# Filler matmuls in the waits of TensorE, and the output bias as a 128-row product, in a fused state-space, attention and feed-forward layer

## The reference

```python
x = x + ssm(_layernorm(x), W_in, conv_w, ..., W_out)      # 512 inner channels, 16 states each
x = x + ffn(_layernorm(x), w_gate, w_up, w_down)          # silu(gate) * up, 768 wide
x = x + wkv(_layernorm(x), Wr, br, Wk, ..., Wo, bo, ...)  # 1024 wide
x = x + ffn(_layernorm(x), w_gate, w_up, w_down)
...
h = scan(exp(dt * A), dt * B * xc)                        # along the 512 tokens, per channel and state
y = (einsum('bldn,bln->bld', h, C) + D * xc) * silu(z)    # the sum over the 16 states
...
out = (sigmoid(R) * WKV).reshape(n, t, -1) @ Wo.T + bo
```

## Time and profile before

| | |
|---|---|
| runs | 1724.32 us median (1724.05, 1724.32, 1731.85) |
| the profiled execution | 1725.72 us, span 1723.9 us |
| mean granted clock of PE | 0.933 |
| busy: PE, DVE, POOL, ACT | 85%, 88%, 73%, 70% of the span |
| memory traffic | 225.20 MB, mean 131 GB/s |

### The profile page before, as it was taken

The page is one execution under the profiler, slowest core; times in us unless marked ns, Lnnn a source line. Parts: engine busy times, 40 slices in busy tenths (PEclk is TensorE's granted clock), DMA queues, the critical chain, the costliest instruction groups (busy, mean ns, idle before and its releaser), DMA issues.

```text
span 1723.9 us, 18980 instructions
## 1 busy us (share of the span) xinstructions
PE 1461.0 (85%) x4800; PEld 713.7 (41%) x4800; DVE 1521.4 (88%) x2045; ACT 1211.0 (70%) x1993; POOL 1265.8 (73%) x970
## 2 busy tenths in 40 slices
PE   5245589779999998899799998899989988999987
PEld 2011234234534552354434453354534553546464
DVE  3399989889999999999999999999999999976561
ACT  3647688856698778968598767889688677664621
POOL 0788987987598877988688867998588978742340
PEclk9567689879999999999899999999999998999999
DMA  8535344324345324453345414553435433321211
GB/s 245 200 110 172 134 141 164 127 92 163 97 145 190 115 100 161 157 175 101 104 139 189 138 56 153 197 193 105 134 121 164 132 119 113 102 63 52 83 49 31
DMA packets 163518, 225.20 MB, mean 131 GB/s; under 512 B 13457, under 2 KB 104082, under 8 KB 163410
## 3 DMA queue, kind: packets, MB, share of 16 engines
q1 hardware_dynamic: 163410, 223.99, 40.0%
HBM read 179.90 MB, written 39.85 MB: 127 GB/s over the span
## 4 chain that ended last, share of the span: by engine, by line
PE 39%; DVE 9%; ACT 6%; issue 5%; POOL 5%; DMA 2%; SPq 1%; DVEq 0%; POOLq 0%; ACTq 0%
PE ps_r L1347 24%; PE ps_r L1356 11%; POOL bu L905 3%; PE ps_y L1398 3%; DVE ps_d L1220 2%; ACT ps_d L1064 1%; DVE bu L1227 1%; ACT L947 1%; DVE sums L1314 1%; PE ps_r L1354 1%; DMA win<-w_in_dram 1%; DVE sums L1308 1%; POOL bu L910 1%; DVE bu L1220 1%; DVE ps_r L1299 1%
## 5 line engine op out<-in xcount | busy, mean ns | idle before, releaser
L905 POOL TENSOR_TENSOR bu<-rep,bc 128x512 f32<-128x512 f32 x512 | 651.2, 1297 | 133.0 <-PE ps_y L1398 114.5
L1064 ACT ACTIVATE ps_d<-rep,scale_a 128x512 f32<-128x512 f32 x512 | 338.1, 684 | 178.5 <-DVE bu L1227 163.4
L1220 DVE TENSOR_TENSOR_SCAN ps_d<-ps_d,bu 128x512 f32<-128x512 f32 x384 | 457.8, 1215 | 6.1 <-ACT ps_d L1064 4.5
L1347 PE MATMUL ps_r<-xT,wgu 128*128 128x512 f32 x768 | 353.5, 606 | 19.4 <-ACT hf L1086 4.5
L1347 PE MATMUL ps_r<-mix,wkv 128*128 128x512 f32 x512 | 250.7, 625 | 32.4 <-DVE yr L1329 8.0
L1227 DVE TENSOR_TENSOR bu<-ps_d,bc 128x512 f32<-128x512 f32 x384 | 251.1, 677 | 0.5
L947 ACT ACT_TABLE_LOAD x191 | 245.1, 1283 | 3.4
L1347 PEld LDWEIGHTS ps_r<-xT,wgu 128*128 128x128 f32 x768 | 142.4, 192 | 225.2 <-issue 215.3
L1398 PE MATMUL ps_y<-bu,sel 128*32 128x512 f32 x1024 | 151.5, 666 | 96.2 <-POOL bu L910 52.9
L922 POOL TENSOR_TENSOR kv<-sums,kv 128x1024 f32<-128x1024 f32 x64 | 150.7, 2355 | 83.7 <-DVE sums L1314 83.3
L910 POOL TENSOR_TENSOR bu<-bu,bc 128x512 f32<-128x512 f32 x128 | 162.7, 1273 | 31.5 <-DVE bu L1220 30.8
(11 more groups left out here) (100 smaller groups left out, 2047.7 us busy)
## 6 DMA issues: line engine op xcount, KB each, us to landing
rep<-dd_scratch SPq DMA_DIRECT2D x128, 512.0 KB, 4.9
wgu<-gu_scratch SPq DMA_DIRECT2D x96, 256.0 KB, 3.3
bc<-bc_scratch SPq DMA_DIRECT2D x64, 256.0 KB, 3.9
dd_scratch<-dd SPq DMA_DIRECT2D x32, 512.0 KB, 3.7
win<-w_in_dram SPq DMA_DIRECT2D x64, 128.0 KB, 2.4
wkv<-w_k_dram SPq DMA_DIRECT2D x64, 128.0 KB, 2.8
wkv<-w_v_dram SPq DMA_DIRECT2D x64, 128.0 KB, 3.2
wr<-w_r_dram SPq DMA_DIRECT2D x64, 128.0 KB, 3.2
```

Source lines behind the costliest of these rows:

```text
L905: pool.tensor_tensor(bu[:, i % BU, :], rep[:, g % REP, 1, :], bc[:, 0, q, :], ALU.mult)\
L1064: act.activation(ps_d[D_BANK[i]][:, :], rep[:, g % REP, 0, :], ACT.Exp, scale=scale_a[:, a, NQ * j + q:NQ * j + q + 1]).then_inc(decay_rea ...
L1220: dve.tensor_tensor_scan(states, d[:, :], bu[:, i % BU, :], 0.0, ALU.mult, ALU.add)\
L1347: last = pe.matmul(dst, lhs, rhs, start=n == 0, stop=n == len(pairs) - 1)
```

## The change

A new unit `p_warm` is put into PE's list, 134 times at 49 places, singly or up to 27 in a row. It multiplies `bo_rows` (128x128, zero but for row 64, which is one) with the first 64 columns of the identity, repeated eight times to 512 columns. Row 64 of those columns is zero, so the product is zero. It is added to `ps_y`, in the middle of an accumulation; ahead of the very first group it opens and closes a sum of its own. The bias becomes the product of `bo_rows` with all 128 rows of `wdt_bo`, whose rows from 64 on are cleared first. The tile `ones` is replaced by a column `one`. The other units, on all engines, keep their order.

```diff
-        wdt_bo = sb("wdt_bo", [RANK + 1, DIN])
+        wdt_bo = sb("wdt_bo", [P, DIN])
...
-        ones = sb("ones", [P, P])
+        one = sb("one", [P, 1])
+        bo_rows = sb("bo_rows", [P, P])
...
+                sp.wait_ge(pool_const.sem, 1)
                 sp.dma_start(bo, b_o).then_inc(r_weights_in.sem, 16)
...
+            pool.memset(wdt_bo[RANK:, :], 0.0).then_inc(pool_const.sem, 1)
+            pool.wait_ge(pool_const.sem, 1)
...
-            pool.memset(ones[:, :], 1.0).then_inc(pool_const.sem, 1)
+            pool.memset(one[:, :], 1.0).then_inc(pool_const.sem, 1)
+            pool.memset(bo_rows[:, :], 0.0).then_inc(pool_const.sem, 1)
...
-            pool.wait_ge(pool_const.sem, 6)
+            pool.wait_ge(pool_const.sem, 8)
+            pool.memset(bo_rows[RANK:RANK + 1, :], 1.0).then_inc(pool_const.sem, 1)
+            pool.wait_ge(pool_const.sem, 9)
...
-                    pe.matmul(d, ones[RANK:RANK + 1, 0:P], bo, start=True, stop=False)
+                    pe.matmul(d, bo_rows[:, :], wdt_bo[:, 0:C], start=True, stop=False)
...
+                    elif unit == "p_warm":
+
+                        if groups and groups % NQ == 0:
+                            pe.wait_ge(gated.sem, at(gated, 0, groups // NQ))
+                        pe.matmul(ps_y[:, :].rearrange("p (a b) -> p a b", b=RANK), bo_rows[:, :],
+                                  ident[:, 0:RANK].unsqueeze(1).to_broadcast([P, T // RANK, RANK]),
+                                  start=groups % NQ == 0, stop=groups % NQ == 0)
                     elif unit == "p_y":
 
+                        groups += 1
```

The list of PE changes only by the inserted words; its first line reads after the change:

```diff
-        "hp_turn*2 p_in*5 p_xproj p_in p_dt p_in*2 p_dt*3 p_y hp_turn*2 p_y p_in*4 p_y*5 p_in*2 p_y p_in*2 p_y "
+        "hp_turn*2 p_in*3 p_warm p_in*2 p_warm*2 p_xproj p_in p_dt p_in*2 p_dt*2 p_warm p_dt p_warm*27 p_y p_warm "
```

More of the change, by code:

```diff
@@ L77 @@
     "rp_turn": KC, "rp_turn2": KC, "rp_up": FM, "rs_ffn": FM, "rv_down": 2, "rv_stats": 2, "rv_aggr": 2, "rv_up": FM,
-    "s_out": 1,
+    "s_out": 1, "p_warm": 1000,
 }
@@ L107 @@
[L107 to L116, removed]
@@ new lines @@
+        "hp_turn*2 p_warm*2 p_y p_warm*2 p_in*4 p_y p_warm*5 p_y*2 p_warm*4 p_y p_warm*8 p_y p_in*2 p_warm*2 p_y "
+        "p_in*2 p_y p_warm*3 p_xproj p_y p_warm p_dt*2 p_y p_warm*7 p_y p_dt*2 p_y p_warm*3 hp_turn p_warm*2 "
+        "hp_turn p_y p_warm*4 p_y p_warm*4 p_y p_post p_y p_post p_warm fp_turn p_warm p_y p_warm*3 fp_turn2 "
+        "p_warm fp_turn fp_turn2 p_y fp_gate fp_up fp_gate p_y fp_up fp_gate fp_up fp_gate p_y fp_up fp_gate "
+        "fp_up p_warm p_y p_warm*2 fp_gate fp_up p_y fp_down fp_down2 p_y fp_down fp_down2 p_in*5 p_y p_in "
@@ new lines @@
+        "fp_turn2 p_in p_y p_in*2 p_wo p_wo2 p_in*3 p_y p_xproj p_k p_v p_dt rp_turn rp_turn2 rp_turn rp_turn2 "
+        "p_y p_recept rp_gate rp_up rp_gate rp_up rp_gate rp_up rp_gate p_y p_warm rp_up p_dt p_y rp_gate*2 "
+        "rp_up*2 p_y p_k rp_down rp_down2 rp_down p_y rp_down2 p_v p_y p_recept*2 p_k*2 p_v*2 p_recept p_y "
+        "p_recept*3 p_k p_warm p_v p_k p_recept p_y p_dt p_k p_v p_post*2 p_v p_wo p_wo2 fp_turn fp_turn2 p_y "
+        "fp_turn fp_turn2 p_wo p_wo2 fp_gate fp_up fp_gate p_y fp_up fp_gate fp_up fp_gate fp_up fp_gate fp_up "
@@ new lines @@
+        "p_y fp_gate fp_up p_k p_dt p_y p_v fp_down fp_down2 fp_down fp_down2 hp_turn*2 p_y p_warm p_wo p_wo2 "
+        "p_wo fp_turn fp_turn2 fp_turn fp_turn2 p_wo2 p_in*2 p_k p_y p_warm p_y p_warm p_in rp_turn rp_turn2 "
+        "rp_turn rp_turn2 p_in*2 p_v p_in*3 p_y p_xproj p_dt p_k p_y p_recept*3 p_v p_k p_v p_dt p_y rp_gate "
+        "p_warm rp_up p_warm p_recept p_y rp_gate rp_up p_k p_v p_recept rp_gate rp_up p_y p_recept rp_gate rp_up "
+        "rp_gate rp_up p_y rp_gate p_recept rp_up p_k p_y rp_down p_v p_recept rp_down2 rp_down p_y rp_down2 p_k "
@@ new lines @@
+        "p_v p_y p_wo p_k p_wo2 p_post*2 p_y p_v p_wo p_wo2 p_dt fp_turn fp_turn2 fp_turn fp_turn2 p_k fp_gate*2 "
+        "fp_up*2 p_y fp_gate fp_up fp_gate fp_up p_y fp_gate fp_up p_dt p_y p_v fp_gate fp_up p_y fp_down "
+        "fp_down2 fp_down hp_turn*2 fp_down2 p_warm p_y p_in p_wo p_wo2 p_y p_wo p_in p_wo2 fp_turn fp_turn2 "
+        "fp_turn fp_turn2 p_in*2 p_warm*2 p_in p_y rp_turn rp_turn2 rp_turn rp_turn2 p_in*2 p_y p_k p_xproj p_v "
+        "p_y p_dt p_in p_recept p_y p_k p_v p_recept*2 rp_gate p_k rp_up p_y rp_gate rp_up p_v p_recept rp_gate "
@@ L443, in full_counts @@
     for seq, unit, i in order("p"):
-        if unit == "p_y" or unit in SECOND.values():
+        if unit in ("p_y", "p_warm") or unit in SECOND.values():
             continue
@@ L1044, in run @@
                             act.wait_ge(m_full.sem, FULL[m, "p_in", 2 * JD - 1])
-                        act.activation(rest_u, dd_slot(i)[:, 1, :], ACT.Identity, bias=ones[:, 0:1]).then_inc(sp_u.sem, 1)
+                        act.activation(rest_u, dd_slot(i)[:, 1, :], ACT.Identity, bias=one[:, 0:1]).then_inc(sp_u.sem, 1)
                         act.wait_ge(sp_u.sem, at(sp_u, m, i + 1))
@@ L1048, in run @@
                         act.wait_ge(sp_ln.sem, at(sp_ln, m, i + 1))
-                        act.activation(rest_u, rest_u, ACT.Identity, bias=ones[:, 0:1], scale=-1.0).then_inc(sp_neg.sem, 1)
+                        act.activation(rest_u, rest_u, ACT.Identity, bias=one[:, 0:1], scale=-1.0).then_inc(sp_neg.sem, 1)
                     elif unit == "a_decay":
@@ L1361, in run @@
             def run(units):
-                dst = {}
+                dst, groups = {}, 0
                 for t, unit, i in units:
```

78 lines of the change are left out of this document (36 added, 42 removed).

## The result

| | before | after |
|---|---|---|
| median of four executions each, taken together | 1727.13 us (1724.05 to 1731.85) | 1701.14 us (1700.30 to 1701.96) |
| ratio | | 0.9847, 95% interval 0.9819 to 0.9875 |
| the profiled execution | 1725.72 us, span 1723.9 | 1701.39 us, span 1699.6 |
| mean granted clock | 0.933 | 0.982 |
| time at the half level, from the clock records | 231.5 us | 62.6 us |

The kernel is 26 us shorter than before by the medians, and 24.3 us between the two profiled executions.

The account below looks back on a forecast made before the run. DVE was taken to bound the long stretch to 1520 us, PE the last. From the profiled 1725.7 us, 1.0 overrun was added, 11.5 clock and 4.1 bias taken off: 1711 us, range 1698 to 1721.

Parts of the forecast that it names:

- The overrun term: Places where a filler ends after the work it stands before is ready: 1 us in all, bounds 0 and 10.
- The clock term: DVE's waits for PE behind half-clock stretches, 80 to 1520 us: full clock wins 11.5 us, ends 0 and 19.4.
- two in or just behind a dip that gets a filler: From 460 to 1520 us, two DVE waits for PE of 1.5 and 2.6 us, 4.1 together, counted as removable.
- six tenths: Share of the 19.4 us of removable waits taken as won, 11.5 us; part would return as waits for POOL or ACT.
- The bias term: 32 biased output tiles, each 0.39 us shorter with the full product: 4.1 us won, ends 0 and 7.2.
- I take 2.5 us: DVE's 11 waits for xk at biased tiles, 5.6 us from 460 to 1520 us: 2.5 us of them won.
- save nothing: In the last stretch, the last four biased tiles, followed by a 4.06 us wait for DVE, win no time.
- The first, off the path: In the long DVE stretch, removed waits for PE become waits for POOL or ACT: 1720 us, chance 0.19.
- The second: Zeros or 32-column groups fail to hold the clock; the first p_y starts 25 us later: 1751 us, chance 0.05.
- The third: Clock held in large gaps only, dips left from 100 to 200 us; half of 11.5 us comes: 1717 us, chance 0.08.
- The fourth: Fillers anywhere delay real work by more than they win, the exposed end of the bounds: 1734 us, chance 0.02.
- What would show it: Signs to check in the new profile: clock, PE busy time, first p_y, biased tile, DVE's waits, last stretch.

Follow-up runs that it names:

- The run with 54 fillers: The changed kernel with 54 instead of 27 fillers ahead of the first p_y: 1719.93 us, ratio 0.9967.
- early and bias: The changed kernel with the 128-row bias and only the 88 fillers up to the 22nd p_y group: 1706.06 us, ratio 0.9902.
- late and bias: The changed kernel with the 128-row bias and only the 46 fillers behind the 30th p_y group: 1706.45 us, ratio 0.9895.
- three places and the bias: The changed kernel with the 128-row bias and only four fillers, at three places in the first 50 us: 1714.38 us, ratio 0.9943.

## Why the prediction was right, and 10 us short

**What bounds the kernel.** DVE's idle time ahead of 1520 us was the right account: of the 51 us in it 21 went (15.7 to 7.8 and 30.0 to 16.9 us), and DVE's busy time fell by 2.3 us only.

**The overrun term**, +1.0, was 1.1 us at the first p_y. The run with 54 fillers shows that an exposed filler costs 0.8 to 0.9 of its length, near to the full length that was named.

**The clock term**, -11.5: the fillers alone gave 17.6, by the interval 14.8 to 20.5. The mechanism was right, DVE's waits for PE behind stretches at half clock, but both of its parts were mis-sized. With the fillers alone, the work that DVE did from 80 to 460 us before takes 6.7 us less (forecast 9.2), and the work from 460 to 1520 us takes 11.2 us less (forecast 2.5); that is one profiled execution of each. Here are waits of DVE for PE, paired one by one, in us. The second column says how far behind the end of the last half-clock stretch DVE went on, by the clock records of before:

| wait, at us before | behind | before | bias alone | fillers alone | early and bias | late and bias | the change |
|---|---|---|---|---|---|---|---|
| xk, 380.9 | 2.6 | 3.8 | 0.7 | 3.5 | 0.7 | 0.6 | 0.7 |
| xk, 455.1 | 1.7 | 1.0 | 1.0 | 0.0 | 1.0 | 0.0 | 0.0 |
| xk, 465.3 | 11.9 | 0.9 | 0.9 | 0.0 | 0.9 | 0.0 | 0.0 |
| ps_y, 857.1 | 0.9 | 1.5 | 1.2 | 0.0 | 1.3 | 0.0 | 0.0 |
| kv, 870.8 | 4.4 | 1.2 | 1.5 | 0.2 | 1.4 | 0.2 | 0.2 |
| kv, 1094.4 | 2.7 | 2.6 | 2.5 | 0.1 | 2.7 | 0.1 | 0.1 |
| ps_y, 1036.0 | 97.9 | 1.0 | 1.0 | 1.0 | 1.0 | 1.0 | 1.0 |
| kv, 1251.8 | 160.2 | 2.1 | 2.2 | 1.7 | 2.7 | 2.3 | 2.8 |

"Most waits for PE fall at full clock and stay" held: see the last two rows. The step that failed is the next one, "two in or just behind a dip that gets a filler", 4.1 us, of which six tenths were taken. Behind 460 us four such waits stood 1 to 12 us behind a half-clock stretch, 0.9 + 1.5 + 1.2 + 2.6 = 6.2 us, and with the fillers 5.9 us of them went, nearly all and not six tenths. A fifth, 1.0 us at 455.1, went with them. DVE's idle time behind 460 us fell by 10.3 us with the fillers alone; the 4.4 us beside the 5.9 are in waits for ACT (5.4 to 3.5 us) and in small ones that differ between executions, and what each of them goes back to stays open.

The late fillers did this, as DVE's waits from 449 to 1502 us in the run of the early version say:

```profile
DVE kv L1300 <- PE ps_r L1356: 5.6, 7, 2.7
DVE xk L1195 <- PE ps_r L1365: 4.1, 6, 1.7
DVE ps_y L1241 <- PE ps_y L1415: 3.7, 6, 1.3
...
DVE kv L1306 <- PE ps_r L1356: 2.9, 2, 2.7
```

The first line is as long with the change (5.2 us); xk falls to 1.4 and ps_y to 1.8 us, and the last line is gone. All of DVE's waits for PE there fall from 17.0 to 9.6 us.

Ahead of 460 us the six tenths were too much, because the largest wait in the sum, 3.8 us of xk at 380.9, was booked on the clock: the fillers alone leave 3.5 us of it. That the whole term still came out within 6.1 us is in part two errors that offset each other.

**The bias term**, -4.1 with the ends 0 and -7.2, measured 9.1 us (by the interval 6.6 to 11.9), above its end. The 0.39 us of a tile were exact; two sizes were wrong. The first is "I take 2.5 us" of the 5.6: the wait of 3.8 us at 380.9 goes to 0.7 with the bias alone, and was not in this sum at all; behind 460 us xk falls from 5.6 to 4.1 us, 1.5 and not 2.5. The second is that the last four biased tiles "save nothing". The wait behind them stays as it is, 4.06 us before, 4.02 with the change and 4.05 with the bias alone:

```profile
1660.19 8.83 PE L1363 MATMUL ps_r<-wo,yr 128*128 128x256 f32 x32 [4.05 <-DVE yr L1336]
```

So all that follows comes 4 x 0.39 = 1.6 us earlier, and the last stretch has 3.1 us of the bias where 1.6 were booked. These three are 3.1 + 1.5 + 3.1 = 7.7 us; the rest is inside what single executions differ by. That the last stretch of the change is nevertheless under 1 us shorter has to do with the clock: behind 1640 us its records show 17.0 us at half level, those of before 10.2 up to the last microsecond, and from the last 32 products of wo to the end it takes 55.5 us instead of 53.4.

Between 80 us and the last stretch DVE waited for xk for 10.3 us before; with the bias alone for 5.8, with three places and the bias for 7.8, with the fillers alone for 7.5, with both for 2.1. The two halves work on the same kind of wait but not on the same waits: the bias ends the one at 380.9, the fillers those at 455.1 and 465.3. That is why they add.

The Trainium skill, TensorE: Matmul & The Clock Gate, Part 2, says that the time of a load of weights goes by its columns and not by its rows. The load records agree: the median is 184 ns for one row and 190 ns for 128. The 0 that the prediction drew from it for this term does not follow: the fillers with the one-row product have 0.9898 and those with the full one 0.9847, and the tile 2.55 and 2.16 us. The extra time stands where products of one row and of 128 meet. In the biased tiles of before, the starts of four records around the one-row product are 309, 320, 304 and 320 ns before the next, those of the others 216; that is the 0.39 us. In the run with one-row fillers two such records of 512 columns in a row start 429 ns apart at full clock, as those with 128 rows do.

**The rivals.** The first, off the path, fell: from 80 to 460 us DVE's waits for POOL went from 5.8 to 6.1 us, where those of the prediction's sum went from 17.2 to 7.2. The second fell in both of its forms, zeros and 32 columns; its price came true in the run with one row. The third was half right about the clock, 0.90 and not 1.00 from 100 to 240 us, with dips of up to 6.8 us, and wrong about the time: DVE was busy for 134 of 140 us there in either case. The fourth is what the 54 fillers show, and the change's 27 stay below it by 1.36 us.

**What would show it**, by number: mean clock 0.98 (0.982); clock 1.00 from 50 to 245 us (it was 1.00 to 100 us, 0.90 from 100 to 240); PE busy 1516 (1530.5); first p_y within 1 us (1.1); biased tile 2.16 (2.16); DVE's waits for PE 6 us (7.2); the last stretch 13 us earlier and 1 to 2 us shorter (24 us earlier and under 1 us shorter).

## What to carry to other kernels

Count what a filler wins at the waits of the engine that bounds the kernel, not by the clock it raises or the gap it fills: here 27 fillers in a gap of 25 us won nothing, and 46 in dips that hardly moved the mean clock won 9 us. To price a dip, list every wait of the bounding engine for PE with its distance behind the last half-clock stretch: here those 1 to 12 us behind one that fillers took away went nearly whole, and those 98 and 160 us behind one stayed. Two edits add when they end different waits, even of one kind, so pair the waits of the versions one by one before a wait is booked on one of them. The edit that saves PE time stops paying once these waits are gone, so try it half and whole.

## What the runs showed of the hardware

- A float32 product with one row in use, put between products of 128 rows of 256 columns, makes an output tile 0.39 us longer: 2.55 against 2.16 us, with and without fillers around it. The time stands at the changes between the two kinds (record starts 304 to 320 ns apart instead of 216). One-row records of 512 columns that follow one another start 429 ns apart at full clock, and 853 at half, and their loads of weights take 184 ns against 190 for 128 rows.
- In the gap ahead of the first p_y, 54 records of 128 rows and 128 columns took 23.44 us and 54 of 32 columns 23.36 us, at full clock, though every product is zero. With one row the clock fell to half behind 51.6 us and stayed there to 119.9 us: 46.44 us for 54 records, at a granted clock of 0.50 with PE busy throughout.
- Early fillers raised the mean clock by 0.032 and won 7.8 us, late ones by 0.013 and won 9.0 us. The mean clock of the version with 54 fillers was 0.976, and it was 18.8 us slower than the change.
- The change's four executions lie within 1.7 us, those of before beside them within 7.8.
